# Softmax sums by products with ones: four attention stages of a decoder kernel

## The reference

```python
# L1_xattn: keys and values of 128 context tokens stand before the 128 of x
attn = jax.nn.softmax(jnp.einsum('bhnd,bhmd->bhnm', q * scale, k), axis=-1)
out = jnp.einsum('bhnm,bhmd->bhnd', attn, v) ; return out @ w_proj.T + b_proj
# L1_ffn (its attention) and L3_attn: causal
scores = jnp.where(mask, -jnp.inf, scores); attn = jax.nn.softmax(scores / np.sqrt(16), axis=-1)
# L2_attn: a bias that falls with the distance of two positions
probs = jax.nn.softmax(scores + bias[None], axis=-1)
```

## Time and profile before

| | |
|---|---|
| median of 3 runs | 3031.39 us (3025.42 to 3032.03) |
| profiled execution | 3037.34 us, span 3035.3 us |
| TensorE busy over the span | 2711.8 us (89%) |
| its weight loads | 2208.2 us (73%) |
| VectorE, ScalarE, GpSimd | 1605.8 (53%), 1413.2 (47%), 1409.6 us (46%) |
| the four stages, from first to last score | 852 to 1110, 1136 to 1316, 1626 to 1798, 2546 to 2715 us |

### The profile page before, as it was taken

How to read it: one execution, slowest core, us unless ns; L and a number is a source line. 1 busy time by engine, 2 the same in 40 slices (tenths; PEclk the granted TensorE clock), 3 DMA queues, 4 the chain that set the end, 5 groups by cost and what they waited for, 6 DMA issues and landing times.

```text
span 3035.3 us, 73536 instructions
## 1 busy us (share of the span) xinstructions
PE 2711.8 (89%) x26345; PEld 2208.2 (73%) x26345; DVE 1605.8 (53%) x3526; ACT 1413.2 (47%) x4543; POOL 1409.6 (46%) x1645
## 2 busy tenths in 40 slices
PE   7889897569989978979996889999997997999999
PEld 6777776446656656658994767878775995768888
DVE  6999999654456655561226763333333004555633
ACT  4666655434456647752226862223322335763310
POOL 3777777633366665543335652323232224663320
PEclk9999999779999999989997989999998998999999
DMA  3000000100000000027652020000005551011100
GB/s 100 3 2 2 2 2 2 56 30 1 24 12 18 14 23 1 0 84 245 238 195 74 0 95 11 8 10 7 10 19 187 186 160 51 0 49 30 53 10 20
DMA packets 96097, 154.50 MB, mean 51 GB/s; under 512 B 12256, under 2 KB 55904, under 8 KB 95600
## 3 DMA queue, kind: packets, MB, share of 16 engines
q1 hardware_dynamic: 89904, 134.92, 13.5%
q0 software_dynamic: 5952, 16.26, 1.5%
HBM read 136.74 MB, written 14.42 MB: 50 GB/s over the span
## 4 chain that ended last, share of the span: by engine, by line
PE 55%; DVE 4%; POOL 4%; issue 3%; ACT 3%; DMA 1%; SPq 0%; DVEq 0%; ACTq 0%; POOLq 0%
PE up_ps L2493 7%; PE e_out_ps L2511 5%; PE t_ps L664 4%; PE s_ps L650 3%; PE bank_a L1557 3%; PE bank_b L1557 3%; POOL probs L569 2%; PE bank_d L701 2%; PE bank_a L612 2%; PE frame_ps L1636 2%; PE bank_b L1573 2%; ACT probs L801 2%; PE bank_d L620 2%; PE bank_a L1573 2%; PE o_ps L690 2%
## 5 line engine op out<-in xcount | busy, mean ns | idle before, releaser
L569 POOL TENSOR_TENSOR probs<-probs,inv 128x512 f32<-128x512 f32 x320 | 328.0, 1039 | 273.6 <-DVE inv L922 273.4
L3454 POOL TENSOR_TENSOR hc<-h,bc 128x1024 f32<-128x1024 f32 x128 | 301.9, 2359 | 113.6 <-DVE h L3735 87.5
L801 ACT ACTIVATE probs<-s_ps,negmax 128x128 f32<-128x128 f32 (+1 forms) x768 | 297.1, 414 | 5.8 <-DVE negmax L882 4.4
L3735 DVE TENSOR_TENSOR_SCAN h<-da,dbu_ps 128x1024 f32<-128x1024 f32 x128 | 292.5, 2285 | 11.2 <-DVE dbu_ps L3747 4.4
L664 PE MATMUL t_ps<-ident,probs 128*128 128x128 f32 x1280 | 209.9, 287 | 60.4 <-POOL probs L569 52.0
L2493 PE MATMUL up_ps<-xT,w_lift 128*128 128x128 f32 x1984 | 233.3, 276 | 0.0
L664 PEld LDWEIGHTS t_ps<-ident,probs 128*128 128x128 f32 x1280 | 140.9, 143 | 127.0 <-POOL probs L569 61.6
L2493 PEld LDWEIGHTS up_ps<-xT,w_lift 128*128 128x128 f32 x1984 | 228.2, 193 | 0.1
L3682 ACT ACTIVATE da<-dta_ps 128x1016 f32<-128x1016 f32 x128 | 130.2, 1018 | 149.7 <-PE dta_ps L3544 149.4
L3544 PE MATMUL dta_ps<-dt,a_spread 32*128 32x128 f32 x2048 | 152.3, 288 | 44.9 <-ACT da L3682 21.0
L882 DVE TENSOR_REDUCE negmax<-s_ps 128x4 f32<-128x1024 f32 (+1 forms) x128 | 156.6, 1223 | 44.1 <-PE s_ps L650 42.1
(11 more groups left out here) (507 smaller groups left out, 6578.6 us busy)
## 6 DMA issues: line engine op xcount, KB each, us to landing
w_lift<-in_L_ffn_w SPq DMA_DIRECT2D x78, 512.0 KB, 4.6
w_lift<-in_L_ffn_w SPq DMA_DIRECT2D x23, 1024.0 KB, 5.1
cT<-in_ctx_turned SPq DMA_DIRECT2D x32, 256.0 KB, 2.6
w_down<-in_L_ffn_w SPq DMA_DIRECT2D x8, 1024.0 KB, 10.5
gathered<-expert_rows_out SPq DMA_DIRECT2D x12, 512.0 KB, 6.4
c_in<-in_ctx SPq DMA_DIRECT2D x16, 256.0 KB, 2.8
w_down<-in_L_ffn_w SPq DMA_DIRECT2D x8, 512.0 KB, 6.1
wkv<-in_L_xattn_Wkv SPq DMA_DIRECT2D x2, 2048.0 KB, 11.7
```

The costliest lines, as they stand in the source:

```text
L569: pool.tensor_tensor(probs[:, u % 2, i], probs[:, u % 2, i], inv[:, u % 2, HB * i:HB * (i + 1)].unsqueeze(2).broadcast_to([P, HB, W]), ALU ...
L801: last = act.activation(probs[:, u % 2, i, k, :], src, ACT.Exp, bias=negmax[:, u % 2, at], accum_out=sums[:, u % 2, at])
L3454: pool.tensor_tensor(hc[:, s % 4], h[:, s % 2], bc[:, j, 1, :].unsqueeze(1).broadcast_to([P, 2 * G, P]), ALU.mult).then_inc(hc_ready.sem, 1)
L3735: dve.tensor_tensor_scan(flat(h[:, s % 2]), flat(da[:, s % 4]), dbu_ps[s % 2][:, :, :, :].rearrange("p i g t -> p (i g t)"), 0.0, ALU.mult ...
```

## The change

The probabilities stay unscaled. GpSimd's `scale` and VectorE's `invert` go, and so do the accumulated sums of the exponentials. `turn_probs` waits for the exponentials alone. `weigh` does each of its products a second time with `counted` in the place of `v`: 32 columns that hold ones for the head of the pair and zeros for the other, so that the second half of `o_ps` receives the sum of a head's probabilities in each of the head's 16 rows. `take_context` takes the reciprocal of that half's chunk, 128x128, and multiplies the chunk by it on the way to `aT`. `counted` is filled by GpSimd where a stage's constants are made.

```diff
-        sums, inv = sb("sums", [P, 2, 2 * HB]), sb("inv", [P, 2, 2 * HB])
+        counted, inv = sb("counted", [P, 2, ROWS]), sb("inv", [P, DC, P])
...
-        per_bank = (exp_done, inv_ready, scaled, p_turned) = (c("exp_done"), c("inv_ready"), c("scaled_done"), c("p_turned"))
-        per_chunk = (a_ready,) = (c("a_ready"),)
+        per_bank = (exp_done, p_turned) = (c("exp_done"), c("p_turned"))
+        per_chunk = (a_ready, inv_ready) = (c("a_ready"), c("inv_ready"))
...
         def constants(pool):
             pool.memset(v[:, :, :, :, :], 0.0).then_inc(consts.sem, 1)
+            pool.memset(counted[:, :, :], 0.0).then_inc(consts.sem, 1)
+            pool.wait_ge(consts.sem, consts.done(1))
+            for par in range(2):
+                pool.memset(counted[:, par, par * HEAD_DIM:(par + 1) * HEAD_DIM], 1.0).then_inc(consts.sem, 1)
             if causal:
                 pool.memset(mask[:, :, :], 0.0).then_inc(consts.sem, 1)
-                pool.wait_ge(consts.sem, consts.done(1))
+                pool.wait_ge(consts.sem, consts.done(4))
                 pool.affine_select(out=mask[:, :, :], in_=mask[:, :, :], compare_op=ALU.is_ge, fill=MASKED, base=0,
...
-            def scale(b, u, i):
-                n = 2 * (NP * b + u) + i
-                pool.wait_ge(inv_ready.sem, inv_ready.done(n))
-                pool.tensor_tensor(probs[:, u % 2, i], probs[:, u % 2, i],
-                                   inv[:, u % 2, HB * i:HB * (i + 1)].unsqueeze(2).broadcast_to([P, HB, W]), ALU.mult
-                                   ).then_inc(scaled.sem, 1)
-
             def unit(b, j, first, left):
                 for u in range(NP):
-                    scale(b, u, 0)
-                    scale(b, u, 1)
...
             def turn_probs(b, u, i):
                 g = NP * b + u
-                pe.wait_ge(scaled.sem, scaled.done(2 * g + i))
+                pe.wait_ge(exp_done.sem, exp_done.done(2 * g + i))
...
                                 last = pe.matmul(o_ps[cg * ROWS:(cg + 1) * ROWS, ch, :],
                                                  v[:, j, t, 4 * ch + cg, par * ROWS:(par + 1) * ROWS],
                                                  pT[:, u % 2, i, k * kt + t, :], start=begins,
+                                                 stop=(par == 1 and t == kt - 1), skip_group_check=True)
+                    for t in range(kt):
+                        for i in banks:
+                            for k, (s, qc, ch, cg, par) in enumerate(pair_heads(kt, u, i)):
+                                last = pe.matmul(o_ps[cg * ROWS:(cg + 1) * ROWS, DC + ch, :], counted[:, par, :],
+                                                 pT[:, u % 2, i, k * kt + t, :], start=False,
                                                  stop=(par == 1 and t == kt - 1), skip_group_check=True)
                 last.then_inc(weighed.sem, 1)
...
             def exponentiate(b, u, i):
                 g = NP * b + u
                 act.wait_ge(negmax_done.sem, negmax_done.done(MAXES * g + (i if alibi else 0)))
-                act.wait_ge(inv_ready.sem, inv_ready.done(2 * (g - 2) + i))
                 act.wait_ge(p_turned.sem, p_turned.done(2 * (g - 2) + i))
                 for k in range(HB):
                     src = biased[:, u % 2, i, k, :] if alibi else s_ps[u % 2][:, i, k * W:(k + 1) * W]
                     at = slice(HB * i + k, HB * i + k + 1)
-                    last = act.activation(probs[:, u % 2, i, k, :], src, ACT.Exp, bias=negmax[:, u % 2, at],
-                                          accum_out=sums[:, u % 2, at])
+                    last = act.activation(probs[:, u % 2, i, k, :], src, ACT.Exp, bias=negmax[:, u % 2, at])
                 last.then_inc(exp_done.sem, 1)
...
             def take_context(b, j, ch):
                 dve.wait_ge(weighed.sem, weighed.done(NP * b + NP - 2 + ch))
+                dve.reciprocal(inv[:, ch, :], o_ps[:, DC + ch, :]).then_inc(inv_ready.sem, 1)
                 dve.wait_ge(out_ready.sem, out_ready.freed(b))
-                dve.tensor_copy(aT[:, j, ch, :], o_ps[:, ch, :]).then_inc(a_ready.sem, 1)
-
-            def invert(b, u, i):
-                g = NP * b + u
-                at = slice(HB * i, HB * (i + 1))
-                dve.wait_ge(exp_done.sem, exp_done.done(2 * g + i))
-                dve.wait_ge(scaled.sem, scaled.done(2 * (g - 2) + i))
-                dve.reciprocal(inv[:, u % 2, at], sums[:, u % 2, at]).then_inc(inv_ready.sem, 1)
+                dve.wait_ge(inv_ready.sem, inv_ready.done(2 * b + ch))
+                dve.tensor_tensor(aT[:, j, ch, :], o_ps[:, ch, :], inv[:, ch, :], ALU.mult).then_inc(a_ready.sem, 1)
...
                         take_context(b - 1, 1 - j, u)
-                    invert(b, u, 0)
                     if u > 0 or not first:
                         copy_probs(*((b, u - 1) if u else (b - 1, NP - 1)))
-                    invert(b, u, 1)
```

More of the change, by code:

```diff
@@ L465, in self_attention_stage @@
         weights = loads.base + 16 * len(plain)
-        ready_consts = consts.base + 1 + (2 if causal else 0)
+        ready_consts = consts.done(3 + (2 if causal else 0))
         v_data = lambda j, t: v[:, j, t].rearrange("p g (two e) -> p g two e", two=2)[:, :, :, 0:HEAD_DIM]
@@ L988, in self_attention_stage @@
         loads.advance(16 * len(plain))
-        consts.advance(1 + (2 if causal else 0))
+        consts.advance(4 + (2 if causal else 0))
         if alibi:
```

## The result

The changed kernel takes 3088.91 us (median of 4 runs, 3085.11 to 3093.74), the kernel before 3031.71 beside it: 1.0192 times as long, 95% interval 1.0175 to 1.021, 57 us more. The forecast was +45, from 3031.39 to 3076: the right way, and 12 us too little. Its profiled execution took 3089.38 us with a span of 3087.6, 52 more than the profiled execution of before. The other 5 us are no work of the kernel's: the profiled execution of before lies 5.6 us above its runs' median, that of the changed kernel 0.5.

What follows compares the result with a forecast made beforehand. TensorE was taken as nearly full (206 of 220 us in the context stage). Context 21, first causal 11, second causal 12, distances 7, ends -6 gave +45 us, a median of 3076 us, range 3030 to 3104.

Steps and rivals of the forecast that it cites:

- The ones on TensorE: All four attention stages: 160 weighings each grow by 0.435 us for the products with ones, 70 us on TensorE.
- The two ScalarE waits: Context stage: two turnings an item wait for ScalarE's copy after a weighing; the longer weighing covers both, -0.44 us.
- The reciprocal: VectorE's context step: 128x128 reciprocal takes 950 ns; with its product VectorE is held 1.18 us, twice an item.
- The rival that asked for 0.56 or less: Faster: all waits go, nothing replaces them, if reciprocal and product hold VectorE at most 0.56 us; -24, 3007 us, chance 0.12.
- the small loss: Rival: reciprocals find cover and the odd copy of turned probabilities comes in time; +14, 3045 us, chance 0.10.
- the worse case: Rival: products with ones don't join the rounds, each weighing takes the block's whole 0.62 more; 3106 us, chance 0.08.
- The odd copy pushed back: Context stage: VectorE's division delays the odd copy of turned probabilities and TensorE's next turning, +0.27 and +0.40 us an item.
- GpSimd's wait before the item's first turning: Context stage: the item's first turning waits 0.47 us for GpSimd, which the change removes, -0.47 an item.
- the context sum: Context stage, growth per item: 1.74 + 0.67 - 0.44 - 0.47 = +1.50 us, x 14 = +21 us.
- the 94 us: Idle time of the turnings' weight loads (L664), 127.0 us less 33.3 of TensorE's own issue: all there is to win.
- the ring of VectorE: Distances stage: VectorE becomes the bound, its chain of work per item 11.48 us against 10.95, +0.53, x 14 = +7 us.
- Ends: Where stages begin and end: small reciprocal's 1.39 us goes, stage ends paid back by longer weighing and context step; together -6 us.

Runs made afterwards that it cites:

- the removal alone: Changed kernel without the products with ones and with a plain copy for the reciprocal, output not divided: 3012.31 us, 0.9919 times the kernel before.

## Why the prediction was right, and where it was off

**The ones on TensorE** were forecast at 0.435 a weighing, 70 us. In the trace the block with ones starts 0.46 after the one with v, and the weighing grows by 0.44. In the causal stages the period grew by 0.81 and 0.87, where the forecast had 0.80 and 0.87. This was right, and it is shown by leaving them out. The two ScalarE waits that they cover, forecast at -0.44, are 0.26 + 0.18 in the kernel of the removal alone, and gone with the ones.

**The reciprocal** was forecast at 0.95 from a straight line between two other shapes, and takes 953 ns. VectorE is held 1.20 us, forecast 1.18. The rival that asked for 0.56 or less fell with this, and so did the small loss, in which the odd copy comes in time; the worse case fell with the 0.46.

**The odd copy pushed back**: in the first quarter +0.27 was forecast and the wait went from 0.55 in the mean to 0.76, +0.21; in the second +0.40, and it went from 0.76 to 1.22, +0.46. Both sums are 0.67; that the two errors of 0.06 cancel is luck. That the copy's place is the reason is shown by the odd copy ahead of the division.

**GpSimd's wait before the item's first turning, -0.47: the term that was mis-sized.** The wait went, but TensorE then came to the query projection before ScalarE had copied x. In the kernel before, the turning waits 0.54 in this item and the projection behind it not at all:

```profile
983.86 0.42 PEld L664 LDWEIGHTS t_ps<-ident,probs 128*128 128x128 f32 x4 [0.54 <-issue]
...
984.24 0.97 PEld L612 LDWEIGHTS bank_a<-xT,wq 128*128 128x128 f32 x8
```

In the changed kernel it is the other way round: the projection at 1012.13 waits 0.35. In the mean of the steady items, the time from the turning of x to the turning of the probabilities fell from 0.69 to 0.27, -0.42, and the time from there to the first key product rose from 1.38 to 1.67, +0.29. Net -0.13. With it the context sum is 1.76 - 0.44 - 0.13 + 0.67 = 1.86 against 1.84 measured, where the forecast had 1.50. The prediction had found this very pair of waits in both causal stages and left it out for the context stage. Turning x earlier took the missing 0.34 away, which shows it. Over 14 items the term is 5 us.

(A smaller slip stands in the period of before, 16.5: the window of the earlier trace rows begins in the middle of a group of key products, no record is missing, and the period is 16.59. And the 94 us that the prediction called all there is to win are an upper bound that was not reached: the removal alone gained 37.)

**Distances**: the ring of VectorE was forecast at 11.48 us and the period is 11.37. Its parts hold: a copy in the reciprocal's place takes 0.67 off, and leaving the ones out takes some 0.4 off the items at a granted clock of 1.00. The growth of 0.53 was reckoned from 10.95, which has the three slow items in it; it is 0.42 from there, and 0.52 from the 10.85 of the others.

**Ends**: forecast -6. From the first to the last key product, the four stages together came out 14.5 us under what 14 steady periods each would add: the first items, bare chains, won more than the 7 or so that I gave them. (2.6 of it is the second period of the distances stage, 13.43 us before, with a wait of 2.63 for GpSimd and a granted clock of 0.64, and 10.81 at 0.85 after; the rest was not taken apart.) But from the last key product on they lost 11 (5.1 in the context stage, 1.5 to 2.5 in the others), where I had the end paid back even. Net -3.5. At the context stage's end both divisions stand on the chain:

```profile
1139.79 0.68 DVE L888 COPY pT<-t_ps 128x512 f32<-128x512 f32 x1
...
1140.62 0.65 PE L685 MATMUL o_ps<-pT,v 128*32 128x128 f32 x16 [1.58 <-DVE pT L888]
...
1143.17 2.07 PE L702 MATMUL bank_d<-wo,aT 128*128 128x256 f32 x4 [1.47 <-DVE aT L916]
```

The last weighing waits 1.58 for the odd copy that stands behind the first division (0.87 before), the output projection 1.47 for the second (0.40 before), and it then takes 2.07 us for what took 1.13 in the kernel before: the granted clock is 0.50 in this stretch, after the idle time, and was 1.00 there before. With the copy in the reciprocal's place 4.6 of these 5.1 us came back.

So the forecast of the profiled time was 7 us low: 5 from the context stage's wait, 2.5 from the ends. The causal stages and the distances nearly cancel. The forecast of the median was 12 low; the other 5 come from taking the profiled execution of before, 6 us above its median, as the measure for the changed kernel too, whose profiled execution lies at its median.

## What to carry to other kernels

Work moved off an engine that was covered (GpSimd's 328 us of scaling here) buys only the waits that it caused: 37 us in this kernel, against some 50 for the sums by TensorE and 36 to 41 for the division. When a wait goes, ask at once which other engine's result the next instruction needs and when that is ready; here 0.29 of 0.42 us came straight back. And where one instruction grows on an engine with its work in a fixed order, look at what stands behind it: putting a short copy in front of it won 0.6 us an item in two stages and lost 0.25 in two others, so the place is chosen stage by stage.

## What the runs showed of the hardware that was not expected

The expert stage behind the first causal one is the same in all kernels, with 1843 TensorE records in each profile, and yet took 291.6 to 303.0 us. Nearly all of the difference lies in its first 60 to 70 us, as windows of the kernel before and of the removal alone show:

```profile
1328.10:1348.90 20.80, 17.42 (x121) 12.62 (x121) 15.64 (x95) 12.72 (x32) 14.09 (x9) 1.00 0.92 297
...
1369.80:1390.60 20.80, 17.36 (x130) 15.38 (x129) 2.50 (x4) 6.30 (x12) 4.79 (x5) 1.00 0.80 269
```

```profile
1305.10:1326.70 21.60, 19.54 (x93) 15.87 (x93) 13.76 (x74) 9.74 (x25) 14.11 (x9) 0.62 0.90 291
...
1348.40:1370.00 21.60, 16.67 (x102) 12.97 (x100) 3.57 (x12) 4.90 (x9) 5.05 (x5) 0.77 0.57 199
```

The granted clock is 1.00 in the one and 0.62 and 0.77 in the other, with 93 records done in the first window and not 121 (in the stretch between the two windows it is 0.59 and 0.58). Kernels with the whole computation took from 292.4 to 299.4 us there, so it is not the data. What in the stages before decides it stays open; it means that 10 us won in one stage can be lost in the next without any wait to show for it, and that stages are best compared by their own spans.
